# Decoder block on one core: the cross-attention's probabilities turned by a transposing DMA instead of by TensorE

## The chip, the cores and the metric

The kernel runs on one core of one Trainium2 chip. The metric is the device time of one execution in microseconds. Engines are called PE (TensorE, with PEld for its weight loads), DVE (VectorE), ACT (ScalarE), POOL (GpSimd) and SP (SyncE, which here only issues DMAs).

## The reference

One decoder block over x of 32 x 64 tokens of 256 values, in three parts, each on a layer norm and with a residual: a self-attention with quantised weights (16 heads of 16), a cross-attention onto a context of 32 x 64 x 128, and a mixture of 8 experts of which each token takes 2. The change lies in the cross-attention:

```python
q = (hidden_states @ Wq).reshape(B, Sq, H, D)          # H = 16 heads, D = 128
k = (encoder_hidden_states @ Wk).reshape(B, Skv, H, D)
v = (encoder_hidden_states @ Wv).reshape(B, Skv, H, D)
q = rmsnorm(q, gq); k = rmsnorm(k, gk)
scores = jnp.einsum('bqhd,bkhd->bhqk', q, k) * scale
attn = jax.nn.softmax(scores, axis=-1)
out = jnp.einsum('bhqk,bkhd->bqhd', attn, v)
return out.reshape(B, Sq, H * D) @ Wo
```

## The kernel before

The kernel has three stages one after the other: attention, cross_attention and experts. Each is written as one list of instructions for each engine, and semaphores order the lists against each other. Matrix products that need more than half precision are made from a high and a low f16 half of each factor, in three terms (TERMS).

In cross_attention the 32 sequences are cut into 4 groups of 8 (NG = 4, 512 tokens, GN). A group has 16 heads, and the work goes over pairs of heads: NPAIR = 32 pairs, 8 a group (NU). The loop variable is N, from -9 to 32. In step N the engines work on several pairs at once:

- PE makes the queries and keys of pair m = N + 9 (query, key and squares, L1209, L1217, L1229), the scores of pair n = N + 1 (scores, L1257), the outputs of the two heads of pair N (attend, L1291) and their way through the output weights (project_out, L1304). Values and output weights were multiplied beforehand, so attend multiplies the probabilities with the context itself.
- DVE turns the scores of pair N + 1 into differences to their maximum (shifted, L1119 to L1123) and sums their exponentials (sums, L1128 to L1132). It makes the low halves of queries (L1099), keys (L1103, L1105) and outputs (out_low, L1109), and of one piece of the experts' weights (L1142).
- ACT makes the exponential (L936), the high halves (out_high, L912, and others), and the copies out of PSUM.
- POOL divides by the sums (quotient, L848) and makes the low half of the probabilities (quotient_low, L853, which raises pl_done), besides products of norms (L841) and one weight piece (L857, L859).
- SP loads and saves pieces of the experts' weights (piece_load, piece_save, L790, L794), and sends the norms of the keys out and back in (L802, L816). It waits in order, so a wait at the head of its step holds up all that stands behind.

Steps 0 to 23 (N < TAIL = 24) are called full here; nearly all of them also make queries and keys. Steps 24 to 31 have only the rest of the attention to do.

PE's order in a full step is: scores(N+1), query(2m), key(2m), turn_p(N), project_out(2N-1), attend(2N), query(2m+1), squares(2m), key(2m+1), project_out(2N), attend(2N+1), squares(2m+1).

For attend the probabilities must lie with the keys on the partitions. turn_p(N) (L1271) does this with eight 128x128 transposes on PE, four blocks of each half, into the PSUM bank that also takes the scores (bank_s), and ACT copies the bank to pT in SBUF (turned_copy, L932). attend(2N) waits for that copy, and scores wait for it before they write the bank again. attend(h) also waits for ol_done, and project_out(h) for the low half of output h.

The experts' stage already turns its inputs by transposing DMAs on SP: rows_in (128x512 f16, L1515) and hid_hl (128x1536 f16, L1522).

Of the kernel before, what the change touches and what calls it, by code (L numbers as in the profile page):

```python
# [7 lines left out]
F16 = mybir.dt.float16  # L8
# [9 lines left out]
P = 128  # L18
# [641 lines left out]
def cross_attention(nc, sem, over, dram, x_sb, cst, ao, hT, wq, wk, wvo, cT, ck, carry, k_hl):  # L660
# [6 lines left out]
    with ctx:  # L667
# [11 lines left out]
        den = [sb(f"x_den{i}", [P, 2 * GT], F32) for i in range(2)]  # L679
        rden = [sb(f"x_rden{i}", [P, 2 * GT], F32) for i in range(2)]  # L680
        p_hl = [sb(f"x_p{i}", [P, 2, GN], F16) for i in range(2)]
        pT = sb("x_pT", [P, 2, 2, 2, P], F16)
        o_hl = [sb(f"x_o{i}", [P, 2, GN], F16) for i in range(2)]
        identh = carry.identh
        qk = pb("xbank_qk", [P, 2, 512], F32)
# [76 lines left out]
        def ob_of(h):  # L762
            return qk if h >= 2 * TAIL - 1 and h % 2 else ob

        def bank_of(n):
            return bank_s if n <= TAIL else bank_n

# [11 lines left out]
        with nc.Block() as block:  # L779

            @block.sync
            def _(sp):
                sp.dma_start(gains[:, 0:1], dram["gq2"].rearrange("(p a) -> p a", a=1)).then_inc(g_in, 16)
                sp.dma_start(gains[:, 1:2], dram["gk2"].rearrange("(p a) -> p a", a=1)).then_inc(g_in, 16)
                def piece_load(i):
                    if i == early:

                        sp.wait_ge(q_done, H2)
                        sp.wait_ge(k_done, H2)
                    sp.dma_start(raw(i), dram["wx"][:, i * PIECE:(i + 1) * PIECE]).then_inc(raw_in[i % 4], 16)  # L790

                def piece_save(i):
                    sp.wait_ge(low_odd if i % 2 else low_even, i // 2 + 1)
                    sp.dma_start(dram["w_hl"][:, :, i * PIECE:(i + 1) * PIECE].rearrange("l p n -> p l n"), halves(i)).then_inc(pair_out[i % 4], 16)  # L794
                    if loaded_behind(i) is not None:
                        piece_load(loaded_behind(i))

                def key_norms_out(b):
                    g, first = b * HB // H2, b * HB % H2
                    sp.wait_ge(kc_done, b + 1)  # L800
                    for t in range(GT):
                        sp.dma_start(dram["key_norms"][g % 2].rearrange("b h t s -> t h b s")[t, first:first + HB],  # L802
                                     kc[32 * t + first:32 * t + first + HB, :].rearrange("h (b s) -> h b s", b=2)).then_inc(kc_saved, 16)

                def key_norms_in(b, part):
                    g, first = b * HB // H2, b * HB % H2
                    sp.wait_ge(kc_saved, (b + 1) * GT * 16)
                    if g:
                        sp.wait_ge(s_read, (b * HB - H2 + HB) // 2)
                    if b == 1:  # L810

                        for r in range(4):
                            sp.wait_ge(pair_out[r], early // 4 * 16)
                    for u in range(first // 2 + 2 * part, first // 2 + 2 * part + 2):
                        for w in range(2):
                            sp.dma_start(rec_k[w * S:w * S + S, 2 * u:2 * u + 2, :].rearrange("p h c -> p (h c)"),  # L816
                                         dram["key_norms"][g % 2, w, 2 * u:2 * u + 2].rearrange("h t s -> (h t s)").partition_broadcast(S)).then_inc(rk_in[u], 16)

                for i in range(4):
                    piece_load(i)  # L820
                for N in steps:
                    for r in range(2):
                        if piece(piece_at(N, r)):
                            piece_save(piece_at(N, r))
                    if batch(N) is not None:
                        key_norms_out(batch(N))
                    for part in range(2):
                        if batch(N - 1 - part) is not None:
                            key_norms_in(batch(N - 1 - part), part)
                for r in range(4):  # L830
                    sp.wait_ge(pair_out[r], (NPIECE + 3 - r) // 4 * 16)
# [64 lines left out]
            def _(act):  # L896
# [31 lines left out]
                                         ACT.Exp, scale=-0.5, bias=gains[:, 4:5]).then_inc(rq_done, 1)  # L928

                def turned_copy(n):  # L930
                    act.wait_ge(t_done, n + 1)
                    nc.scalar.copy(pT[:, :, :, :, :].rearrange("p e l a n -> p (e l a n)"), bank_s[:, :].bitcast(F16)).then_inc(pT_done, 1)  # L932

                def exponent(n):
                    act.wait_ge(sub_done, n + 1)
# [1 line left out]

                def quotient_high(n):
                    act.wait_ge(pf_done, n + 1)
                    nc.scalar.copy(p_hl[n % 2][:, 0, :], pf[:, :, :].rearrange("p a s -> p (a s)")).then_inc(ph_done, 1)  # L940

                def piece_high(i):
# [44 lines left out]
                for N in steps:  # L987
# [22 lines left out]
                        query_norms(batch(N))  # L1010
                    if pair(m):
                        key(2 * m)
                    if pair(N):
                        turned_copy(N)
                    if pair(n):
                        exponent(n)
                    if pair(N):
# [184 lines left out]
            def _(pe):  # L1202
# [35 lines left out]
                def scores(n):  # L1238
                    pe.wait_ge(lq_done, n * 2 + 2)
                    pe.wait_ge(lk_done, n * 2 + 2)  # L1240
                    if n == 1:
                        pe.wait_ge(s_read, 1)
                    if 1 < n <= TAIL:
                        pe.wait_ge(pT_done, n - 1)
                    if n == TAIL + 1:

                        pe.wait_ge(rq_done, NHEAD // HB)
# [11 lines left out]

                def turn_p(n):  # L1260
                    pe.wait_ge(pl_done, n + 1)
                    if n < TAIL:

                        pe.wait_ge(s_read, n + 2)
                    else:
                        pe.wait_ge(pT_done, n)
                    for e in range(2):
                        for l in range(2):
                            for a in range(2):
                                at = (e * 2 + l) * 2 + a  # L1270
                                last = nc.tensor.transpose(bank_s[:, :].bitcast(F16)[:, at * P:(at + 1) * P], p_hl[n % 2][:, l, e * RW + a * P:e * RW + (a + 1) * P], identh[:, :])  # L1271
                    last.then_inc(t_done, 1)

                def attend(h):
                    pe.wait_ge(pT_done, h // 2 + 1)
                    if h == 2 * TAIL - 1:

                        pe.wait_ge(lq_done, NHEAD)
# [6 lines left out]
                    for a in range(2):  # L1285
                        for b in range(2):
                            for j, (l, m) in enumerate(TERMS):
                                for half in range(2):
                                    rows = slice(half * S, half * S + S)
                                    at = (2 * a + b) * S  # L1290
                                    last = nc.tensor.matmul(bank[:, half, at:at + S], ck[rows, l, h // H2 * 2 + a, b * CC:(b + 1) * CC],  # L1291
                                                            pT[rows, h % 2, m, a, b * S:b * S + S], start=(j == 0), stop=(j == 2))
                    last.then_inc(o_done, 1)

                def project_out(h):
# [44 lines left out]
                for N in steps:  # L1340
# [32 lines left out]
                        turn_hidden(6)  # L1373
                    if m == 6:
                        turn_hidden(7)
                    if pair(N):
                        turn_p(N)
                    if head(2 * N - 1):
                        project_out(2 * N - 1)
                    if pair(N):  # L1380
# [569 lines left out]
```

## Time and profile before

| | us |
|---|---|
| median of 3 runs | 901.29 |
| lowest, highest | 898.33, 901.67 |
| the profiled execution | 901.22 |
| its span, first to last instruction | 899.4 |
| mean granted TensorE clock | 0.936 of full speed |
| PE busy | 759.5 (84%) |
| DVE busy | 610.2 (68%) |
| ACT busy | 492.5 (55%) |
| POOL busy | 381.7 (42%) |

Busy times are sums over the span. Matmuls overlap in the pipeline, so a busy PE is not one at its peak. The full steps of the cross-attention lie from about 282 to 538 us, the experts' stage behind 597 us.

### The profile page before, as it was taken

How to read it: one execution, taken by the hardware profiler on the slowest of the kernel's cores; microseconds unless marked ns; L12 is line 12 of the kernel's file. 1: busy time of each engine (PE TensorE's matmuls, PEld its weight loads, DVE VectorE, ACT ScalarE, POOL GpSimd, SP SyncE). 2: the span in 40 equal slices, each digit the busy share in tenths (PEclk: the TensorE clock that was granted, in tenths of full speed). 3: DMA queues.
4: the chain of work that ended last, by engine and by line, in shares of the span. 5: the costliest groups of instructions: out<-in, count | busy, mean ns of one | idle time of the engine just before them, and what ended most of it. 6: DMA issues, size and time to landing. Idle time of an engine off the chain costs nothing. (4 is left out here: it accounts for less than half of the span.)

```text
span 899.4 us, 27604 instructions
## 1 busy us (share of the span) xinstructions
PE 759.5 (84%) x11193; PEld 544.5 (61%) x11193; DVE 610.2 (68%) x1069; ACT 492.5 (55%) x923; POOL 381.7 (42%) x446
## 2 busy tenths in 40 slices
PE   0498888887888999899999996985479999999991
PEld 0497787885444666566656665855247777777770
DVE  6778898864899999899999997967723333333330
ACT  0677777764877777676767764533023333333330
POOL 0123222222356555455555556510225666656642
PEclk9889988886999999999999997997689999999996
DMA  9100000001365333333334443149958899988874
GB/s 324 66 27 26 28 30 22 26 27 34 121 200 158 127 120 119 120 119 120 118 120 120 120 126 100 39 147 420 399 99 141 144 144 144 144 138 149 142 114 119
DMA packets 141226, 112.37 MB, mean 125 GB/s; under 512 B 88592, under 2 KB 121488, under 8 KB 140912
## 3 DMA queue, kind: packets, MB, share of 16 engines
q1 hardware_dynamic: 124672, 88.32, 36.8%
q0 software_dynamic: 7488, 10.23, 7.5%
q10 hardware_dynamic: 8944, 12.06, 3.9%
q8 instruction: 93, 1.52, 0.7%
q14 instruction: 29, 0.24, 0.1%
HBM read 63.13 MB, written 29.10 MB: 103 GB/s over the span
## 5 line engine op out<-in xcount | busy, mean ns | idle before, releaser
L1747 DVE SCALAR_TENSOR_TENSOR f_slot_work<-psu,f_slot_work 128x688 f32<-128x688 f32 x39 | 34.1, 874 | 124.0 <-PE psu L1818 124.0
L1304 PE MATMUL xbank_a<-arena,x_o 128*128 128x256 f16 x768 | 96.8, 277 | 8.1 <-DVE x_o L1109 6.4
L1566 POOL DMA_INDIRECT token_out<-f_y,f_to x39 | 62.2, 1594 | 79.9 <-ACT f_y L1622 54.3
L1304 PEld LDWEIGHTS xbank_a<-arena,x_o 128*128 128x128 f16 x768 | 71.8, 99 | 28.5 <-DVE x_o L1109 17.7
L1209 PE MATMUL xbank_qk<-arena 128*128 128x512 f16 x336 | 83.5, 385 | 1.7 <-DVE q_hl L1099 1.7
L1818 PE MATMUL psg<-wgu,f_slot_work 128*128 x468 | 76.7, 315 | 9.2 <-DMA f_slot_work<-rows_in 9.2
L1835 PE MATMUL fbank<-arena,f_slot_work 128*128 (+1 forms) x663 | 82.7, 273 | 0.5 <-DMA f_slot_work<-hid_hl 0.5
L848 POOL TENSOR_TENSOR x_pf<-x_sc,x_rden 128x512 f32<-128x512 f32 x32 | 33.4, 1042 | 108.3 <-DVE x_rden L1132 108.3
L1835 PEld LDWEIGHTS fbank<-arena,f_slot_work 128*128 128x128 f16 (+1 forms) x663 | 64.4, 97 | 18.9 <-issue 8.9
L1818 PE MATMUL psu<-wgu,f_slot_work 128*128 x468 | 75.1, 310 | 0.0
L1614 ACT CAST hid_hl<-f_slot_work 128x688 f16<-128x688 f32 x39 | 29.8, 765 | 77.8 <-DVE f_slot_work L1747 77.8
L901 ACT ACTIVATE sqq<-xbank_qk 128x512 f32<-128x512 f32 x56 | 33.3, 595 | 58.1 <-PE xbank_qk L1209 58.1
L1607 ACT ACTIVATE f_slot_work<-psg 128x688 f32<-128x688 f32 x39 | 29.0, 743 | 65.8 <-PE psg L1818 63.0
L1818 PEld LDWEIGHTS psg<-wgu,f_slot_work 128*128 128x128 f16 x468 | 43.2, 99 | 33.9 <-issue 10.0
L1818 PEld LDWEIGHTS psu<-wgu,f_slot_work 128*128 128x128 f16 x468 | 46.0, 98 | 22.9
L1750 DVE TENSOR_TENSOR hid_hl<-f_slot_work,hid_hl 128x688 f16<-128x688 f32 x39 | 34.1, 875 | 32.4 <-ACT hid_hl L1614 32.4
L528 PE MATMUL bank_pt<-cst,sp 64*64 64x64 f32 x1024 | 43.1, 244 | 14.3 <-ACT pT L289 13.7
L208 POOL TENSOR_SCALAR kd<-cst,deq 128x128 f32<-128x128 f32 x16 | 12.2, 764 | 95.6 <-PE bank_g L574 67.0
L1109 DVE SCALAR_TENSOR_TENSOR x_o<-xbank_o,x_o 128x512 f16<-128x512 f32 x55 | 37.7, 685 | 17.3 <-ACT x_o L912 17.3
L528 PEld LDWEIGHTS bank_pt<-cst,sp 64*64 64x64 f32 x1024 | 38.9, 156 | 16.3 <-issue 14.7
L1209 PEld LDWEIGHTS xbank_qk<-arena 128*128 128x128 f16 x336 | 28.6, 98 | 32.7 <-DVE q_hl L1099 2.5
L1217 PE MATMUL xbank_qk<-cT,wk 128*128 128x512 f16 x168 | 46.0, 383 | 0.0
(297 smaller groups left out, 1880.9 us busy)
## 6 DMA issues: line engine op xcount, KB each, us to landing
arena<-in_wx SPq DMA_DIRECT2D x51, 256.0 KB, 3.9
wgu<-w_hl SPq DMA_DIRECT2D x2, 5504.0 KB, 29.9
ao<-key_norms SPq DMA_DIRECT2D x64, 128.0 KB, 3.8
w_hl<-cT SPq DMA_DIRECT2D x26, 256.0 KB, 2.1
w_hl<-x_pair SPq DMA_DIRECT2D x25, 256.0 KB, 3.3
arena<-w_hl ACTq DMA_DIRECT2D x1, 3072.0 KB, 19.9
ao<-in_wx SPq DMA_DIRECT2D x10, 256.0 KB, 3.7
w_hl<-ao SPq DMA_DIRECT2D x10, 256.0 KB, 2.6
```

The lines of the kernel that those rows point to most:

```text
L528: last = nc.tensor.matmul(pt[rows, n * S:(n + 1) * S], sp[i % 2][rows, 8 * part + n, :], cst[rows, IDENT + S * b:IDENT + S * b + S], start ...
L848: nc.gpsimd.tensor_tensor(pf[:, :, :], sc[n % 2][:, :, :], rden[n % 2][:, :].unsqueeze(2).to_broadcast([P, 2 * GT, S]), ALU.mult).then_inc ...
L901: nc.scalar.activation(sqq[h % 2][:, :], query_bank(h), ACT.Square, scale=1.0 / (H_UP * W_UP)).then_inc(sq_done, 1)
L1109: nc.vector.scalar_tensor_tensor(out=o_hl[h % 2][:, 1, :].rearrange("p (b n) -> p b n", b=2), in0=ob_of(h)[:, :, 0:RW], scalar=1.0 / P_UP, ...
L1209: last = nc.tensor.matmul(query_bank(h), wq[:, a, k, f:f + D2], hT[:, g, b * NCH + k, :], start=(j == 0), stop=(j == len(terms) - 1))
L1217: last = nc.tensor.matmul(key_bank(h), wk[:, a, f:f + D2], cT[:, g, b, :], start=(j == 0), stop=(j == 2))
L1304: last = nc.tensor.matmul(acc[t // 2][:, (t % 2) * C:(t % 2 + 1) * C], o_hl[h % 2][:, a, at:at + P], wvo[:, b, e, :], start=(e == 0 and j ...
L1566: nc.gpsimd.indirect_dma_start(out=dram["token_out"], out_offset=bass.IndirectOffsetOnAxis(ap=to[n % 2][:, 0:1], axis=0), in_=y[n % 2][:, ...
L1747: nc.vector.scalar_tensor_tensor(out=h3, in0=psu[:, :].rearrange("p (c n) -> p c n", c=2)[:, :, 0:FH], scalar=HID_UP / (H_UP * W_UP), in1= ...
L1750: nc.vector.tensor_tensor(hid_hl[n % 2][:, 1, 0:FF], hid[n % 2][:, :], hid_hl[n % 2][:, 0, 0:FF], ALU.subtract).then_inc(s["hh_low"], 1)
L1818: last = nc.tensor.matmul(bank[:, c * 512:c * 512 + FH], xT[n % 2][:, b * NCH + k, :], wgu[:, bass.ds(e, 1), at:at + FH].rearrange("p a n ...
L1835: last = nc.tensor.matmul(ps[n % 2][:, 0:C], hidT[n % 3][0:rows, a, f, :], wd[0:rows, bass.ds(e, 1), at:at + C].rearrange("p a n -> p (a n)"),
```

## The change

The full steps' probabilities are turned by one DMA a pair, issued on SP at the head of SP's step N. The PE transposes and the ACT copy of these steps are gone; the eight tail steps keep them. The DMA has two destination buffers. The second lies in hT[:, 1], the hidden states of group 1, which are no longer read once the queries of that group are made; it takes the odd pairs from pair 9 on, and pT_first takes all others. Each parity of the pair has a semaphore of its own (turned_in). The order of the blocks in a buffer is changed from (head, half) to (half, head). scores(n) now waits only until the scores before are read (s_read), and quotient_high(n) waits until the transposition of pair n - 2 has read its buffer.

```diff
-        pT = sb("x_pT", [P, 2, 2, 2, P], F16)
+        pT_first = sb("x_pT", [P, 2, 2, 2, P], F16)
+        pT_second = hT[:, 1].rearrange("p j n -> p (j n)")[:, 0:8 * P].rearrange("p (l e a n) -> p l e a n", l=2, e=2, a=2)
+        turned_in = [sem(f"x_turned_in{i}") for i in range(2)]
...
+        def second(n):
+            return n % 2 == 1 and NU < n < TAIL
+
+        def pT_of(n):
+            return pT_second if second(n) else pT_first
+
+        def reader_before(n):
+
+            return max((k for k in range(n) if second(k) == second(n)), default=-1)
+
+        def turned_count(n):
+            return 16 * (n // 2 + 1)
...
+                def turn_p(n):
+                    sp.wait_ge(pl_done, n + 1)
+                    if reader_before(n) >= 0:
+                        sp.wait_ge(o_done, 2 * reader_before(n) + 2)
+                    if second(n):
+                        sp.wait_ge(q_done, 2 * H2)
+                    sp.dma_start(pT_of(n)[:, :, :, :, :].rearrange("p l e a n -> p (l e a) n"), p_hl[n % 2][:, :, :].rearrange("p l n -> p (l n)"), transpose=True).then_inc(turned_in[n % 2], 16)
+
                 for N in steps:
+                    if pair(N) and N < TAIL:
+                        turn_p(N)
                     for r in range(2):
...
                 def quotient_high(n):
                     act.wait_ge(pf_done, n + 1)
+                    if 2 <= n < TAIL + 2:
+                        act.wait_ge(turned_in[n % 2], turned_count(n - 2))
...
-                    if pair(N):
-                        turned_copy(N)
                     if pair(n):
                         exponent(n)
...
-                    if n == 1:
-                        pe.wait_ge(s_read, 1)
-                    if 1 < n <= TAIL:
-                        pe.wait_ge(pT_done, n - 1)
+                    if 1 <= n <= TAIL:
+                        pe.wait_ge(s_read, n)
...
                 def attend(h):
-                    pe.wait_ge(pT_done, h // 2 + 1)
+                    if h < 2 * TAIL:
+                        pe.wait_ge(turned_in[h // 2 % 2], turned_count(h // 2))
+                    else:
+                        pe.wait_ge(pT_done, h // 2 - TAIL + 1)
...
-                    if pair(N):
-                        turn_p(N)
                     if head(2 * N - 1):
                         project_out(2 * N - 1)
```

## Rows read from the trace of the kernel before

**Rows 1.** The page: TensorE's granted clock, in tenths, in 40 slices.

```profile
PEclk9889988886999999999999997997689999999996
```

**Rows 2.** Windows: window, length, busy PE, PEld, DVE, ACT, POOL (count), clock, DMA share.

```profile
392.00:478.00 86.00, 82.16 (x1383) 52.12 (x1380) 79.17 (x121) 60.58 (x108) 45.22 (x40) 1.00 0.38 120
```

**Rows 3.** Timeline of DVE in one full step, its window, all of L1123.

```profile
413.68 0.69 DVE L1109 SCALAR_TENSOR_TENSOR x_o<-xbank_o,x_o 128x512 f16<-128x512 f32 x1 [0.41 <-ACT x_o L912]
414.50 0.69 DVE L1119 TENSOR_TENSOR x_sc<-xbank_s,ao 128x512 f32<-128x512 f32 x1
...
421.12 0.68 DVE L1109 SCALAR_TENSOR_TENSOR x_o<-xbank_o,x_o 128x512 f16<-128x512 f32 x1
...
424.48 0.69 DVE L1109 SCALAR_TENSOR_TENSOR x_o<-xbank_o,x_o 128x512 f16<-128x512 f32 x1 [0.58 <-ACT x_o L912]
...
414.50:421.10 6.60, 6.43 (x77) 3.70 (x77) 6.42 (x10) 4.30 (x8) 2.40 (x2) 1.00 0.29 90
...
L1123 DVE TENSOR_TENSOR x_sc<-x_sc,x_mx x22: 691/1578/1649, 305.9 to 536.1; 128x512 f32<-128x512 f32 x22
```

**Rows 4.** Timeline of PE and ACT in the same step.

```profile
416.35 0.61 PE L1271 MATMUL xbank_s<-identh,x_p 128*128 128x128 f16 x8
...
416.79 1.47 PE L1304 MATMUL xbank_a<-arena,x_o 128*128 128x256 f16 x12
...
418.43 0.52 PE L1291 MATMUL xbank_o<-x_pT,ck 64*128 64x64 f16 x24 [0.17 <-ACT x_pT L932]
...
421.86 1.49 PE L1304 MATMUL xbank_a<-arena,x_o 128*128 128x256 f16 x12 [0.17 <-DVE x_o L1109]
...
423.28 0.52 PE L1291 MATMUL xbank_o<-x_pT,ck 64*128 64x64 f16 x24
...
423.85 0.60 ACT L912 ACTIVATE x_o<-xbank_o 128x512 f16<-128x512 f32 x1 [0.33 <-PE xbank_o L1291]
```

**Rows 5.** The same step: POOL's x_p, SP's first issue, a window.

```profile
412.51 1.16 POOL L853 TENSOR_TENSOR x_p<-x_pf,x_p 128x512 f16<-128x512 f32 x1
...
418.16 0.38 SPq L794 DMA_DIRECT2D w_hl<-cT  x1
...
413.70:417.70 4.00, 4.00 (x74) 2.79 (x69) 3.80 (x5) 2.27 (x5) 2.65 (x2) 1.00 0.00 0
```

**Rows 6.** Timeline of the experts' stage: transposing DMAs and their waiters.

```profile
656.35 1.20 SPq L1515 DMA_TRANSPOSE f_slot_work<-rows_in  x1
...
658.82 0.18 POOL L1548 COPY f_at<-f_from_all 128x1 uint32<-128x1 uint32 x1 [0.44 <-DMA f_slot_work<-rows_in]
...
873.86 1.42 SPq L1522 DMA_TRANSPOSE f_slot_work<-hid_hl  x1
...
877.77 2.14 PE L1835 MATMUL fbank<-arena,f_slot_work 128*128 x17 [0.54 <-DMA f_slot_work<-hid_hl]
...
693.14 1.19 SPq L1515 DMA_TRANSPOSE f_slot_work<-rows_in  x1
...
698.87 0.18 POOL L1548 COPY f_at<-f_from_all 128x1 uint32<-128x1 uint32 x1 [0.49 <-DMA f_slot_work<-rows_in]
```

**Rows 7.** Timeline of steps 0 and 23 and the step behind.

```profile
282.66 1.17 POOL L853 TENSOR_TENSOR x_p<-x_pf,x_p 128x512 f16<-128x512 f32 x1
...
287.05 0.52 PE L1291 MATMUL xbank_o<-x_pT,ck 64*128 64x64 f16 x24 [1.48 <-ACT x_pT L932]
...
532.67 1.16 POOL L853 TENSOR_TENSOR x_p<-x_pf,x_p 128x512 f16<-128x512 f32 x1
...
537.34 0.53 PE L1291 MATMUL xbank_o<-x_pT,ck 64*128 64x64 f16 x24
...
542.80 1.03 PE L1271 MATMUL xbank_s<-identh,x_p 128*128 128x128 f16 x8 [3.71 <-POOL x_p L853]
```

**Rows 8.** Windows of the filling steps and of the attention stage.

```profile
274.00:278.00 4.00, 2.43 (x14) 0.84 (x10) 3.90 (x7) 2.98 (x8) 2.21 (x2) 1.00 0.06 21
132.00:133.00 1.00, 0.00 (x0) 0.00 (x0) 1.00 (x1) 0.94 (x6) 1.00 (x1) 0.61 0.00 0
```

More of the change, by code:

```diff
@@ L930, in turned_copy @@
                 def turned_copy(n):
-                    act.wait_ge(t_done, n + 1)
-                    nc.scalar.copy(pT[:, :, :, :, :].rearrange("p e l a n -> p (e l a n)"), bank_s[:, :].bitcast(F16)).then_inc(pT_done, 1)
+                    act.wait_ge(t_done, n - TAIL + 1)
+                    nc.scalar.copy(pT_first[:, :, :, :, :].rearrange("p l e a n -> p (l e a n)"), bank_s[:, :].bitcast(F16)).then_inc(pT_done, 1)
                 def exponent(n):
@@ L1261, in turn_p @@
                     pe.wait_ge(pl_done, n + 1)
-                    if n < TAIL:
-                        pe.wait_ge(s_read, n + 2)
+                    if n == TAIL:
+                        pe.wait_ge(s_read, TAIL + 1)
                     else:
-                        pe.wait_ge(pT_done, n)
+                        pe.wait_ge(pT_done, n - TAIL)
                     for e in range(2):
@@ L1269, in turn_p @@
                             for a in range(2):
-                                at = (e * 2 + l) * 2 + a
+                                at = (l * 2 + e) * 2 + a
                                 last = nc.tensor.transpose(bank_s[:, :].bitcast(F16)[:, at * P:(at + 1) * P], p_hl[n % 2][:, l, e * RW + a * P:e * RW + (a + 1) * P], identh[:, :])
@@ L1291, in attend @@
                                     last = nc.tensor.matmul(bank[:, half, at:at + S], ck[rows, l, h // H2 * 2 + a, b * CC:(b + 1) * CC],
-                                                            pT[rows, h % 2, m, a, b * S:b * S + S], start=(j == 0), stop=(j == 2))
+                                                            pT_of(h // 2)[rows, m, h % 2, a, b * S:b * S + S], start=(j == 0), stop=(j == 2))
                     last.then_inc(o_done, 1)
```

## The prediction

> **What bounds the kernel now.** I read the page first, for where the stage lies and at what clock TensorE runs in it [rows 1]: slices 14 to 24 of the forty, where PE and DVE show eights and nines, are the stage that the change touches, and the granted clock is nine tenths or more there. The view by windows over 86 us of it has PE busy 82.16 us, DVE 79.17 and ACT 60.58 [rows 2]. PE at 96% and DVE at 92% are too close for shares to decide, and a busy PE in this view is not one at its peak. So I laid out one full step (one pair of heads, N in the code) in order of time, first DVE, then PE.
>
> DVE first [rows 3]. A step repeats after 10.80 us: out_low(2N+1) at 413.68 and again at 424.48. The scores are read at 414.50 (L1119), and from there to out_low(2N) at 421.12 DVE works its list without a pause: 6.42 us busy in a window of 6.60 us, and the 0.18 us left over are the hand-overs between dependent instructions. The 1.58 us of L1123 belong to that list. Both times out_low(2N+1) had to wait, 0.41 and 0.58 us, for ScalarE's out_high (L912).
>
> PE after that [rows 4]. Behind out_low(2N), which ends at 421.12 + 0.68 = 421.80, project_out(2N) starts at 421.86, attend(2N+1) at 423.28, ScalarE's out_high(2N+1) at 423.85, DVE's out_low(2N+1) at 424.48. So the loop that sets the step is: DVE list 6.62 us (414.50 to 421.12), out_low 0.68, hand-over 0.06, project_out 1.42 to the start of attend, attend with hand-over 0.57, ScalarE 0.63, then out_low(2N+1) 0.69 and 0.13 to the next L1119: 6.62 + 0.68 + 0.06 + 1.42 + 0.57 + 0.63 + 0.69 + 0.13 = 10.80 us. In it PE has no part but project_out(2N) and attend(2N+1), in the second half. The eight transposes (start 416.35) and the first attend (418.43) lie in the first half, beside the DVE list. PE paid for them with its own slack only: project_out(2N) is released by DVE's out_low after 0.17 us of idle PE.
>
> **What the change removes.** In each of the 24 full steps the eight PE transposes go. They hold PE from 416.35 to the start of project_out(2N-1) at 416.79, so 0.44 us [rows 4]. The wait of attend(2N) for ScalarE's copy, 0.17 us, goes too if the DMA is in time. PE thus comes to project_out(2N) some 0.6 us earlier and finds out_low(2N) not done: its idle time there grows from 0.17 to about 0.8 us. Worth on the path: 0. Without that cover it would be 24 x 0.61 = 14.6 us.
>
> ScalarE loses one copy of 128x1024 a step, which runs between the last transpose and attend(2N). Its result is only wanted by attend. The work behind it on ScalarE is the exponent and out_high(2N), and DVE takes both only when its list, gapless as it is, comes to them. Worth: 0. Also 0 are the freed score bank (scores(N+1) waits for an older reader than before, but PE arrives there late, behind squares and attend(2N+1), at the end of the loop), the second buffer, and the new wait of quotient_high for a transposition two steps old, 21 us back. The wait for the queries of the second group is over by step 9, the first that uses the second buffer (the last of those queries is made in step 6).
>
> **What it adds.** One transposing DMA of 128x1024 f16 (256 KB, eight blocks) on SP's queue, at the head of SP's step, after pl_done(N). That is the end of x_p's low half on POOL: 412.51 + 1.16 = 413.67 [rows 5]. The other wait, for the reader of the same buffer, is met earlier: attend(2N-1) starts a period before the 423.28 of attend(2N+1), at 412.48, and hands over within 0.57 us, by 413.05. From step 10 on the reader is two steps back.
>
> How late may it land? attend(2N) started at 418.43 with 0.17 us to spare before project_out(2N) had its input, so up to 418.60 costs nothing: a budget of 418.60 - 413.67 = 4.93 us. PE itself would now be at attend(2N) at 418.43 - 0.61 = 417.8, 4.15 us after pl_done.
>
> How long does it take? The trace has transposing DMAs in the experts' stage only [rows 6]. 128 KB on nearly idle engines: issued 656.35, its waiter on POOL starts at 658.82: 2.47 us. 384 KB beside a scatter: issued 873.86, its waiter on PE starts at 877.77: 3.91 us. 128 KB beside the DMAs of the other slots: 693.14 to 698.87: 5.73 us. In the full steps the engines are idle when the transposition would run: the DMA share is 0.00 over 413.7 to 417.7 [rows 5]. So I interpolate between the first two: (2.47 + 3.91) / 2 = 3.2 us. Bounds are 2.5 and 5.7 us. At 3.2 us it lands at 416.9, 0.9 us before PE arrives and 1.7 us inside the budget. I take 0 per step; the upper bound gives 5.73 - 4.93 = 0.80 us a step, 19 us in all.
>
> The Trainium skill ("VectorE: DVE Perf Modes", section "The three transpose paths") speaks against the change: it gives 1309 ns for one 128x128 block through the DMA crossbar against 390 ns on TensorE, and advises TensorE where the result may go to PSUM. Eight blocks one after another would be 10.5 us by that page, an estimate, and the sum would be 901.3 + 24 x (10.5 - 4.9) = some 1035 us. The row of 384 KB, twelve blocks in 3.91 us with issue and landing, disagrees with such an addition.
>
> What stands behind the new instruction on SP: the two saves and two loads of weight pieces and, in two steps of four, the four loads of key norms. The first of them is issued at 418.16 [rows 5], when DVE has the even piece ready, while the transposition's issue (1.20 to 1.42 us [rows 6]) is over by 415.2. Nothing is held up: 0.
>
> **The edges.** Step 0: x_p is ready at 282.66 + 1.17 = 283.83 and attend(0) starts at 287.05 after a wait of 1.48 us for the copy [rows 7]. With 3.2 us the DMA lands at 287.1: 0 to +0.3 us. Step 23, which has no query and key projections to hide behind: x_p at 532.67 + 1.16 = 533.83, attend(46) at 537.34 [rows 7]. The DMA lands at 537.1, and attend(46) starts then, 0.2 us earlier; it is worth 0, for PE stands idle 3.71 us a little later, until POOL has the next x_p at 542.8. The eight tail steps keep the old way.
>
> **The sum.** Profiled execution 901.22 us (span 899.4, 1.8 around it), which is the median of the three runs, 901.29, to 0.1. Removed on the path 0, added 0, edges 0 +- 0.3: **901.3 us**.
>
> **Rivals.**
> A. PE's time counts after all, because DVE's list has slack that the view does not show. For it: PE is busy 96% and out_low waits 0.4 to 0.6 us in each step. Against it: these waits lie behind project_out(2N), which starts 0.06 us after DVE's out_low ends. Full price -14.6 us: 886.6. If only a part counts, 890 to 897. Put under A as well: DVE's L1123 takes 1.58 us in the median and 0.69 at its shortest [rows 3]. Were it always short, that would be 24 x 0.89 = -21 us, 880; but nothing that starts DVE's or POOL's instructions there moves.
> B. (the other side) The transposition lands late and its wait takes the place of the copy's. It decides from 4.93 us after pl_done; each 0.25 us beyond is 6 us on the total, so 907 at 5.2 us and 920 at the 5.73 us of the loaded row. For it: the trace has no transposition of 256 KB, and the key norms' DMAs end only a few us before. Against it: idle engines in the very window.
> C. PE idles more and the granted clock falls to the lower level. In the filling steps 4 us with PE busy 2.43 keep 1.00, while a drop (0.61 in that us) comes in a stretch without any PE work [rows 8]. The new idle pieces are some 0.8 us long. If the whole stage ran at half the clock, its PE work, 10.0 us a step, would double: at least 24 x 9 = +216 us, 1117.
> D. The blocks of one transposition are done one after another, each at the price of the loaded row: 5.73 / 4 = 1.43 us. Eight would take 11.5 us, 6.5 beyond the budget: +157 us, 1058. Against it stands the row of twelve blocks in 3.91 us. (The Trainium skill's "VectorE: DVE Perf Modes", named above, has a block price of that size; the trace disagrees with its addition.)
> That the DMA isn't made, or that the old way stays, can't be: the code for N < TAIL has no other.
>
> **Chances.** No change 0.70, A 0.12, B 0.14, C 0.03, D 0.01. A measurement of this kernel can tell about 0.5%, 4.5 us, from no change; its three runs spread over 3.3 us. The likeliest case's own range is 898 to 905. Range for 8 in 10: all of it, the mild half of A and of B: 894 to 908. Faster by over 0.5%: 0.12; within: 0.71; slower: 0.17.
>
> **What would show it.** Right: the step still repeats after 10.8 us; DVE busy 6.4 of 6.6 us between L1119 and out_low(2N); PE's idle time before project_out(2N) grown to about 0.8 us with DVE's out_low as releaser; attend(2N) with no wait, or a short one, for the transposing DMA; landing 3 to 3.5 us after x_p. Wrong: attend's waits for the DMA longer than 0.8 us (B), a step shorter than 10.5 us (A), a granted clock under 1.00 in these slices (C). The prediction fails most easily on the one size that has no row, the landing of 256 KB, and on the reading that DVE's list has no slack.

## The result and the profile after

| | before | after |
|---|---|---|
| median of 11 runs each, us | 899.02 | 896.02 |
| lowest, us | 896.73 | 894.11 |
| the profiled execution, its span, us | 901.22, 899.4 | 894.42, 892.6 |

The ratio is 0.9967, with a 95% interval of 0.9954 to 0.998: the changed kernel is faster by 0.33%. That is under the 0.5% which the prediction named as the least that can be told, but more runs than the three of before told it. One of the eleven runs of the kernel before, 1019.67 us, was a slow one, which the ratio leaves out. Of the 5.3 us between forecast and measurement, 2.3 us are the kernel before, which took 899.02 us in these runs and not 901.29; 3.0 us are the change.

The page after, beside [rows 1]: busy times, the granted clock, and two DMA queues (packets, MB, share).

```profile
PE 744.8 (83%) x11001; PEld 530.0 (59%) x11001; DVE 607.6 (68%) x1069; ACT 472.3 (53%) x899; POOL 382.7 (43%) x446
...
PEclk9999888886999999999999998997689999999996
...
q1 hardware_dynamic: 150016, 94.62, 42.7%
...
q8 instruction: 92, 1.51, 0.7%
```

PE lost 192 matmuls and as many weight loads, ScalarE 24 copies, 20.2 us of busy time. The clock is nine tenths or more in the stage, so rival C is out. The last line becomes important below: q8 brings in instructions, one packet of 16 KB at a time (1.51 MB / 92).

One full step after: DVE, timeline, beside [rows 3].

```profile
411.21 0.69 DVE L1144 TENSOR_TENSOR x_sc<-xbank_s,ao 128x512 f32<-128x512 f32 x1
411.93 0.69 DVE L1146 TENSOR_REDUCE x_mx<-x_sc 128x8 f32<-128x512 f32 x1
412.65 1.58 DVE L1148 TENSOR_TENSOR x_sc<-x_sc,x_mx 128x512 f32<-128x512 f32 x1
414.16 0.68 DVE L1167 SCALAR_TENSOR_TENSOR cT<-arena,cT 128x512 f16<-128x512 f32 x1
...
417.82 0.68 DVE L1134 SCALAR_TENSOR_TENSOR x_o<-xbank_o,x_o 128x512 f16<-128x512 f32 x1
...
421.18 0.69 DVE L1134 SCALAR_TENSOR_TENSOR x_o<-xbank_o,x_o 128x512 f16<-128x512 f32 x1 [0.63 <-ACT x_o L937]
422.00 0.69 DVE L1144 TENSOR_TENSOR x_sc<-xbank_s,ao 128x512 f32<-128x512 f32 x1
```

The scores are read at 411.21 and again at 422.00: 10.79 us, as before (10.80). The list from there to out_low(2N) takes 417.82 - 411.21 = 6.61 us (6.62 before). L1148 is the old L1123, still 1.58 us.

The same step on PE, beside [rows 4].

```profile
414.46 0.52 PE L1317 MATMUL xbank_o<-x_pT,ck 64*128 64x64 f16 x24
415.49 1.47 PE L1234 MATMUL xbank_qk<-arena 128*128 128x512 f16 x6 [0.51 <-DVE q_hl L1124]
...
418.56 1.49 PE L1330 MATMUL xbank_a<-arena,x_o 128*128 128x256 f16 x12 [0.27 <-DVE x_o L1134]
419.98 0.52 PE L1317 MATMUL xbank_o<-x_pT,ck 64*128 64x64 f16 x24
```

attend(2N) comes 3.25 us behind the read of the scores (3.93 before), without a wait. The freed time came out as idle time, 0.51 us ahead of the next query and 0.27 us ahead of project_out(2N): 0.78 us in all, where the prediction had 0.8, but all of it ahead of project_out(2N). In this step the loop therefore did what was forecast. To find the 3 us I cut the two profiled executions into stages by their first and last instructions: the 24 full steps (from the first read of the scores to the 25th) took 260.50 us before and 258.84 after, the tail up to the statistics 62.09 and 60.20, the experts' slots (first to last sigmoid-weighted gate on ScalarE) 208.74 and 207.38. These two executions differ by more than the medians, 6.8 us in the span, and 2.5 us of that lie ahead of the first full step (274.15 and 271.61 us), where nothing was changed. Two single places hold the differences of tail and slots.

Place 1, the tail's third step, whose scores are read 546.64 and 557.70 before (11.06 us), 542.45 and 551.60 after (9.15 us). Before: SP's load of a weight piece, ScalarE's wait for it.

```profile
551.16 2.08 SPq L790 DMA_DIRECT2D arena<-in_wx  x1
...
555.94 0.63 ACT L948 ACTIVATE cT<-arena 128x512 f16<-128x512 f32 x1 [5.59 <-DMA arena<-in_wx]
```

After:

```profile
546.97 0.47 SPq L805 DMA_DIRECT2D arena<-in_wx  x1
...
549.84 0.63 ACT L975 ACTIVATE cT<-arena 128x512 f16<-128x512 f32 x1 [3.68 <-DMA arena<-in_wx]
```

The same load is issued in 2.08 us before and in 0.47 us after; ScalarE and everything behind it waits 1.91 us less. The DMA view of the kernel before for 550.5 to 552.0 us names who else is there (an instruction packet, and no such line for 546.0 to 547.5 us after):

```profile
q8 instruction: 1, 0.02, 6.2%
...
arena<-in_wx SPq DMA_DIRECT2D x1, 256.0 KB, 4.8
```

Place 2, the third slot of the experts: 4.86 us from gate to gate before, 3.50 us after. Before, the turned rows come late for PE:

```profile
668.05 1.19 SPq L1515 DMA_TRANSPOSE f_slot_work<-rows_in  x1
...
672.69 1.92 PE L1818 MATMUL psg<-wgu,f_slot_work 128*128 x12 [1.22 <-DMA f_slot_work<-rows_in]
```

After, the same DMA issued at 662.12 is waited for by nobody on PE. Here too the DMA view has an instruction packet in the kernel before, 1.5 us behind the issue, and none after.

### The profile page after: what moved, and what is told of

Read it like the earlier page. It is cut to its first block and busy times, and to the rows that moved or that the text cites. A ratio compares the mean times of both kernels' runs of the same rounds, so it can differ in the third digit from the quotient of the medians.

```text
span 892.6 us, 27243 instructions
## 1 busy us (share of the span) xinstructions
PE 744.8 (83%) x11001; PEld 530.0 (59%) x11001; DVE 607.6 (68%) x1069; ACT 472.3 (53%) x899; POOL 382.7 (43%) x446
## 3 DMA queue, kind: packets, MB, share of 16 engines
q8 instruction: 92, 1.51, 0.7%
```

## The experiments

My first theory, from these two places: PE's instruction stream is 384 instructions shorter by the tail (192 matmuls and 192 weight loads). The packets therefore fall at other moments (one and a half packets, if a packet holds 256 instructions, as the page of the Trainium skill named below has it), and no longer beside two DMAs whose landing is on the path. Against it stood: PE's and ScalarE's freed time, the transposing DMA itself, and chance.

All runs in one table: median, ratio to the kernel before among the same runs with its 95% interval, and from the profile the 24 full steps, the tail's third step and the experts' third slot.

| kernel | us | ratio | steps | tail | slot |
|---|---|---|---|---|---|
| before | 899.02 | 1 | 260.50 | 11.06 | 4.86 |
| before_again | 898.87 (one run) | | 259.73 | 10.15 | 5.20 |
| after | 896.02 | 0.9967 (0.9954 to 0.998) | 258.84 | 9.15 | 3.50 |
| after_again | 896.82 | 0.996 (0.9944 to 0.9976) | 258.58 | 9.14 | 3.50 |
| no_turn | 896.41 | 0.997 (0.9952 to 0.9989) | 257.08 | 9.15 | 3.50 |
| dma_alone | 898.25 | 0.9978 (0.9959 to 0.9998) | 259.93 | 10.35 | 4.90 |
| dma_alone2 | 900.64 | 1.0007 (0.9989 to 1.0025) | 259.78 | 9.93 | 4.95 |
| pad_before | 897.44 | 0.9986 (0.9968 to 1.0003) | 259.47 | 9.16 | 3.50 |
| pad_after | 897.08 | 0.9972 (0.9958 to 0.9986) | 256.42 | 10.04 | 3.50 |
| pad2_before | 899.49 | 0.9997 (0.9977 to 1.0016) | 262.27 | 9.66 | 4.97 |
| pad2_after | 896.70 | 0.9966 (0.9949 to 0.9983) | 257.85 | 9.12 | 3.50 |
| port_before | 892.77 | 0.9919 (0.9896 to 0.9942) | 254.15 | 9.78 | 5.05 |
| port_after | 889.88 | 0.9883 (0.9859 to 0.9907) | 250.41 | 9.10 | 3.50 |
| port2_before | 892.57 | 0.9927 (0.9907 to 0.9948) | 251.36 | 10.22 | 4.80 |
| port2_after | 886.84 | 0.9869 (0.9843 to 0.9895) | 247.31 | 9.24 | 3.50 |
| late_in | 898.94 | 0.9994 (0.9975 to 1.0013) | 260.09 | 9.18 | 3.50 |
| late_out | 905.15 | 1.0065 (1.0043 to 1.0087) | 266.48 | 9.16 | 3.50 |

### The two kernels once more, and each half of the change

after_again and before_again are the two kernels unchanged.

> The changed kernel once more, for a second trace. Its first trace keeps the full step at 10.79 to 10.80 us, yet its median is 3.0 us under the kernel before. Theory S (steps): the loop through DVE is unchanged and the 3 us come from single places: late loads of weight pieces in steps 9, 22 and 27, and stages outside the cross-attention, where two executions of one kernel differ as much. Then the places differ from trace to trace and the period stays 10.80. Theory R (real, at an edge): the same places gain again, above all the tail step 27, where 1.9 us were gained. Ratio to before in both 0.995 to 0.999.

> The kernel before once more, for a second trace. Theory S: the steps with a late weight piece lie elsewhere than in its first trace (steps 9 and 27), the period is 10.8 us elsewhere, and the attention stage differs from the first trace by 1 to 3 us. Theory R: step 27 is again some 2 us longer than in the changed kernel.

no_turn has neither the transposes nor the DMA: each later full pair's attend reads the probabilities that were turned in step 0.

```diff
                     if pair(m):
                         key(2 * m)
-                    if pair(N):
+                    if N == 0:
                         turned_copy(N)
...
-                    pe.wait_ge(pT_done, h // 2 + 1)
+                    pe.wait_ge(pT_done, 1 if h < 2 * TAIL else h // 2 - TAIL + 2)
```

> The kernel before without the PE transposes and ACT copies of the full steps 1 to 23; attend reads the probabilities that step 0 turned, so the output is not the reference's. No DMA takes their place. If DVE sets the step as predicted: period 10.8 us, time within 0.3% of before, that is 897 to 901 us. If PE's 0.6 us a step count: 885 us. If the 3 us of the change come from the freed PE and ACT time, this shows them too, with 895 to 897 us.

dma_alone (and later dma_alone2, the same) is the kernel before with the new DMA for pairs 9 to 23 beside the old way, into a buffer that nobody reads.

```diff
+                    if NU < N < TAIL:
+                        turn_p(N)
```

> The kernel before with all its work, and beside it the transposing DMA of pairs 9 to 23 into the second buffer, which nobody reads (15 of the 24, for there is no room for the first nine). If DMA and queue cost nothing: 899 us, period 10.8. If the DMA delays pieces or engines: over 900 us, with DMA waits of ACT for pieces. If the DMA in some way brings the gain (for instance by moving the loads of pieces): 895 to 897 us.

Leaving the turning out altogether gains no more than moving it to the DMA: 0.997 against 0.996 and 0.9967. So the DMA costs nothing beyond these intervals, about 2 us on the whole (single late landings do cost something, below), and the gain belongs to the removal. Most steps repeat after 10.79 to 10.80 us in all of them. What goes with the removal in these profiles is the tail's third step and the slot. dma_alone was unclear: its profile has both stalls, its ratio was a little below 1. The repetition below gives 1.0007.

### Where the instruction packets fall

pad_before and pad_after put 64 tiny matmuls ahead of PE's first work, where it waits for data until 13.57 us anyway: 128 instructions, half a packet.

```diff
+                pad = cst[:, 0:P].bitcast(F16)
+                for i in range(64):
+                    nc.tensor.matmul(kb[:, 0:4], pad[:, 0:P], pad[:, P:P + 4], start=True, stop=True)
```

> The kernel before with 64 tiny matmuls (64 weight loads and 64 matmuls of 4 columns) ahead of its first work on PE, into a bank that is written afterwards; 128 PE instructions more, about 5 us of PE at the most, in a time in which PE waits for its first data. Nothing else is changed. Theory 1 (the place of the instruction loads): the packets of 16 KB by which instructions are brought in come once per 256 PE instructions, so they now fall half a period elsewhere. Then the one beside SP's load in the tail goes: the 27th step from its scores to the next takes 9.15 us in place of 10.2 to 11.1, and the third slot of the experts 3.50 us in place of 4.9 to 5.2. In all 1 to 3 us less than before, 896 to 898 us, ratio 0.996 to 0.999. Theory 2 (the gain is PE's and ScalarE's freed time, or the freed copy): nothing moves, 899 to 900 us, and both steps keep their old lengths.

> The changed kernel with the same 64 tiny matmuls ahead of its first work on PE. Theory 1 (the place of the instruction loads): the packets fall near where they fell before, so the 27th step takes 10 us or more again and the third slot of the experts about 4.9 us; 898 to 900 us, ratio to the kernel before 0.999 to 1.001. Theory 2 (freed time of PE and ScalarE): the gain stays, 896 to 897 us, ratio 0.996 to 0.997, the 27th step at 9.15 us and the third slot at 3.50 us.

pad2_before and pad2_after have 128 of them, a whole packet.

> The kernel before with 128 tiny matmuls ahead of its first work on PE: 256 PE instructions, a whole period of the instruction loads, so that these fall where they fell before. It is the control of pad_before. Theory 1 (the place of the instruction loads): the tail's 27th step takes 10.2 to 11.1 us again and the third slot of the experts 4.9 to 5.2 us; 899 to 900 us, ratio 0.999 to 1.001. Theory 2 (the tiny matmuls did something of their own, such as a warmer PE): both stay at 9.15 and 3.50 us, as in pad_before, 897 us.

> The changed kernel with 128 tiny matmuls, a whole period. Theory 1 (the place of the instruction loads): 9.15 us for the 27th step and 3.50 us for the third slot as in the changed kernel; 896 to 897 us, ratio 0.996 to 0.997. Theory 2 (any padding costs something): 897 to 898 us, like pad_after.

> The kernel before with transposing DMAs of pairs 9 to 23 into a buffer that nobody reads, once more, since its first ratio of 0.9978 left open whether the DMA by itself gains something. Theory 1 (place of the instruction loads, and steps that PE without transposes can shorten): neither is changed, ratio 0.999 to 1.001, the 27th step above 10 us and the third slot 4.9 us. Theory 2 (the DMA beside the old way gains by itself): ratio 0.998 or less again.

In the tail theory 1 held in all four. The padding by half a packet freed the kernel before (9.16 us) and loaded the changed one (10.04 us); the whole packet did neither (9.66 and 9.12 us). This is pad_after, the changed kernel with the stall put back: the issue is long, ScalarE waits 0.9 us more.

```profile
546.43 1.28 SPq L808 DMA_DIRECT2D arena<-in_wx  x1
...
550.19 0.63 ACT L978 ACTIVATE cT<-arena 128x512 f16<-128x512 f32 x1 [4.56 <-DMA arena<-in_wx]
```

The DMA view in windows of 0.1 us gives each packet's place. In eight of the 17 profiles a packet lies between 0.5 us ahead of the start of this load's issue and 0.5 us behind it; the step takes 9.66 to 11.06 us in them (mean 10.15), and the issue 0.89 to 2.08 us in seven of the eight. In the nine others no packet is there, the issue takes 0.47 us and the step 9.10 to 9.24 (mean 9.16). The price of this place is 1.0 us. The same holds for the weight loads of the whole cross-attention in all 17 profiles: without a packet within 0.5 us of its start the issue took more than 0.6 us in 23 of 786 cases, with one in 48 of 81. The number of q8's packets follows PE's instructions too: 93 before, 94 in both of its paddings, 92 after.

The expectation for pad_after failed in two points: its slot took 3.50 us, not 4.9, and its time came out at 897.08 us, ratio 0.9972, and not at 898 to 900. By the time alone theory 2 (896 to 897 us) would have been nearer. The positions account for the slot. In the seven profiles with the long slot (4.80 to 5.20 us) a packet follows the issue of the rows' DMA by 1.4 to 2.1 us. In pad_after it follows by 2.3 us, and the rows were no longer delayed; in pad_before, and in the profiles without PE transposes other than pad_after, there is none. In pad_before the rows of the next slot came late instead: issued at 665.81 us, they reached PE at 671.42, with a packet 3.4 us behind their issue, and that slot took 6.48 us in place of 5.57. How near a packet must lie to delay a landing is therefore not told by these profiles. So pad_before gave back 0.9 us of what it gained, and pad_after lost only the tail: the ratios of both lie between those of the two kernels, where the whole packets reproduce these (0.9997 and 0.9966). The intervals of the half paddings overlap, so single medians don't separate them; the steps in the profiles do.

The Trainium skill, "Runtime: NRT & Kernel Launch", section "Instruction fetch mechanics", says that instructions are refilled in blocks of 16 KiB, 256 instructions, and that crossing a block is mostly hidden. The size agrees with q8's packets. For the DMAs issued beside it the fetch was not hidden: the load's issue took 0.89 to 2.08 us in place of 0.47 in seven profiles. What it cost PE itself no row here shows.

### What the change is worth when DVE's list is shorter

Rival A rested on slack in DVE's list, L1123's 1.58 us above all. In the traces of both kernels it takes that long where POOL's second operation on its weight piece has started before it (412.53 to 413.69 us beside the list above), and 0.69 us where it starts first itself (in the kernel before at 295.01, POOL 0.01 us later) or where POOL's second operation comes later still. That holds for all 391 of these subtractions in steps 1 to 23 of the 17 profiles: 1.57 to 1.68 us in 221 of them, 0.69 us in 168 of the 170 others. port_before and port_after hold POOL's piece until DVE has the block maximum; port2_before and port2_after until DVE has done its own weight piece too.

```diff
                     n, m = N + 1, N + AHEAD
+                    if pair(n) and N < TAIL:
+                        pool.wait_ge(mx_done, n + 1)
```

```diff
+                        if piece(piece_at(N, 0)):
+                            pool.wait_ge(low_even, piece_at(N, 0) // 2 + 1)
+                        else:
+                            pool.wait_ge(mx_done, n + 1)
```

> The kernel before, with one wait more on POOL: in a full step whose successor begins a pair, POOL holds its next weight piece until DVE has left the block maximum of the step after. This keeps POOL's two-input operation off the time in which DVE's two-input operations on SBUF take 1.58 us instead of 0.7. Theory 1 (DVE's list holds a recoverable collision of about 0.9 us a step, and PE with its eight transposes is the next limit): full steps of about 10.3 us in place of 10.80, 24 x 0.5 = 12 us less, 887 us, range 884 to 892. Theory 2 (the list has no slack to be had, or POOL's piece then comes late): steps of 10.80 us or more, 899 us or above.

> The changed kernel with the same wait on POOL. Theory 1: without the collision the step is set by PE, which has no transposes here: steps of about 9.95 us, 24 x 0.85 = 20 us less than the changed kernel, 877 us, range 873 to 883, and so 8 to 10 us under the kernel before with the same wait: this is what the change is worth where DVE no longer sets the step. Theory 2 (no recoverable collision): 896 us or above. Theory 3 (collision gone, but the transposes' 0.44 us a step were hidden on PE all the same): the same time as the kernel before with this wait, within 2 us.

The collision was recoverable, but both sizes were off: steps of 10.45 and 10.32 us (10.3 and 9.95 expected), so the change was worth 0.13 us a step. In port_after DVE's list is still the bound, 6.15 us with the weight piece at 1.10 us beside POOL's:

```profile
410.05 0.69 DVE L1146 TENSOR_TENSOR x_sc<-xbank_s,ao 128x512 f32<-128x512 f32 x1
...
411.50 0.69 DVE L1150 TENSOR_TENSOR x_sc<-x_sc,x_mx 128x512 f32<-128x512 f32 x1
...
412.11 1.10 DVE L1169 SCALAR_TENSOR_TENSOR cT<-arena,cT 128x512 f16<-128x512 f32 x1
...
416.20 0.68 DVE L1136 SCALAR_TENSOR_TENSOR x_o<-xbank_o,x_o 128x512 f16<-128x512 f32 x1
```

6.15 us and the same 4.17 us behind it are 10.32. That gave the next two expectations.

> The kernel before with POOL's next weight piece held until DVE has finished its own weight piece of the step (in place of the block maximum, as in port_before). In port_before DVE's piece still took 1.10 us beside POOL's, and 0.68 without it, but there PE, with its eight transposes a step, went without a pause. Theory 1 (PE with the transposes sets 10.44 us there): the 0.42 us taken from DVE's list are worth nothing, steps stay at 10.4 to 10.45 us, 892 to 893 us. Theory 2 (DVE's list still sets the step): 10.0 us, 24 x 0.4 = 10 us less, 883 us.

> The changed kernel with the same hold on POOL. In port_after the step of 10.32 us is DVE's list of 6.15 us and the same 4.17 us behind it as in the kernel before, with PE idle 0.28 us ahead of project_out. Theory 1 (DVE's list still sets it, PE has some 0.3 us of room without the transposes): the list falls by 0.42 to 5.7 us and PE takes over at 10.32 - 0.28 = 10.0 us; 22 x 0.3 = 7 us less than port_after, 883 us, range 881 to 886. The change is then worth some 0.4 us a step, 9 to 10 us, against the kernel before with the same hold. Theory 2 (PE limits both at 10.3 to 10.4 us): 889 to 890 us, and the change is worth 3 us at any length of DVE's list.

Now the steps came close to the expectations: 10.45 us with the transposes, 9.90 to 9.91 without (10.0 expected). port2_after's time, 886.84 us, lies above its range of 881 to 886. The windows of one such step, columns as in [rows 2], first port2_before:

```profile
418.41:428.86 10.45, 10.28 (x179) 6.71 (x179) 9.13 (x16) 7.42 (x13) 5.86 (x5) 1.00 0.51 158
```

then port2_after:

```profile
477.16:487.06 9.90, 9.90 (x172) 6.31 (x171) 9.12 (x15) 7.02 (x15) 5.83 (x5) 1.00 0.64 137
```

PE is busy 10.28 us and waits 0.17 us for ScalarE's copy in the first, and works without any pause in the second. PE is now the bound, and the change is worth 0.38 us of PE's work (10.28 - 9.90) and the 0.17 us of waiting, 0.55 us a step, against 0.61 in the prediction for the case without cover. Yet the medians differ by 5.7 us, not 24 x 0.55 = 13. Four of the steps could gain nothing: 0, 1, 9 and 17 take 9.0, 10.5, 11.1 and 11.1 us in both. port2_after's other rows tell where 6.3 us more went: attend waits for late transpositions.

```profile
383.14 1.24 SPq L840 DMA_TRANSPOSE x_pT<-x_p  x1
...
389.68 0.52 PE L1322 MATMUL xbank_o<-x_pT,ck 64*128 64x64 f16 x24 [2.42 <-DMA x_pT<-x_p]
```

This landing took 6.54 us, with an instruction packet 2.2 us behind the issue; that step lasted 12.25 us. Three more late landings (5.47, 5.72 and 4.72 us; behind the second a packet lies only at 3.6 us) made steps of 11.13, 12.09 and 10.43 us: together 2.35 + 1.23 + 2.19 + 0.53 = 6.3 us over 9.90.

### How late may the transposition land?

late_in and late_out issue the DMA of steps 0 to 22 only behind DVE's read of the next scores (s_read), or behind its maximum (mx_done).

```diff
+                    if n + 1 < TAIL:
+                        sp.wait_ge(s_read, n + 2)
                     sp.dma_start(pT_of(n)...
```

> The changed kernel with each transposition of steps 0 to 22 issued only after DVE has read the next pair's scores, some 1.5 us later than x_p is ready. It then lands 3.15 us after that, 3.9 us behind the start of the read; attend(2N) may start 4.1 us behind it (418.60 - 414.50 in the kernel before). Theory 1 (the budget of 4.93 us behind x_p holds): the step stays 10.80 us and the time 896 to 897 us. Theory 2 (the budget is smaller, PE must come to attend earlier): steps over 10.9 us and 900 us or more.

> The changed kernel with each transposition of steps 0 to 22 issued only after DVE's block maximum, 0.72 us later again. It lands 4.6 us behind the start of the read of the scores, 0.5 us after the budget. Theory 1: a new loop sets the step: read of the scores and maximum 1.45 us, landing 3.15, attend(2N) and the queries and keys up to project_out(2N) 3.3, project_out 1.42, attend and hand-over 0.57, ScalarE 0.63, out_low and hand-over 0.82: 11.3 us, 23 x 0.5 = 12 us more, 908 us, range 903 to 915. Theory 2 (PE's time freed by the transposes covers it): 10.80 us and 896 to 897 us.

late_in kept its step of 10.79 us, with attend waiting some 0.5 us, though its median came out at 898.94, 2 us above the expectation; its interval reaches down to 0.9975 and its profile shows only 1.3 us more in the full steps than after's. late_out has the new loop in every step, 11.09 to 11.13 us (11.3 expected) and 905.15 us (908). On PE and SP in late_out:

```profile
418.64 1.24 SPq L842 DMA_TRANSPOSE x_pT<-x_p  x1
```

```profile
421.74 0.52 PE L1319 MATMUL xbank_o<-x_pT,ck 64*128 64x64 f16 x24 [1.28 <-DMA x_pT<-x_p]
424.83 1.47 PE L1332 MATMUL xbank_a<-arena,x_o 128*128 128x256 f16 x12
```

The landing is 3.10 us, 4.60 us behind the start of the read of the scores at 417.14. That costs 0.3 us a step, and late_in's 3.88 us (412.71 + 3.10 - 411.93) cost nothing. So attend may come some 4.3 us behind the read, where the prediction had 4.1 (418.60 - 414.50): rival B's mechanism exists, and its budget was right to 0.2 us.

## Why the prediction was right, and where it failed

- The loop of 10.80 us was right in each of its parts for most steps: period 10.79, DVE's list 6.61, PE's freed 0.78 us turned into waits for DVE. Taking DVE's list away (port2) moved the bound to PE, as that reading says.
- "Removed on the path 0" was right for most steps, not for all. Where a weight piece for ScalarE came late, POOL's piece moved and missed DVE's: "nothing that starts DVE's or POOL's instructions there moves" was too strong. The changed kernel shows one such step, on DVE and POOL:

```profile
510.67 1.49 POOL L882 TENSOR_SCALAR arena<-arena 128x512 f32<-128x512 f32 x1 [1.92 <-ACT x_pair L975]
511.02 0.80 DVE L1148 TENSOR_TENSOR x_sc<-x_sc,x_mx 128x512 f32<-128x512 f32 x1
512.24 1.20 POOL L884 TENSOR_TENSOR x_pair<-arena,x_pair 128x512 f16<-128x512 f32 x1
```

  That step took 10.01 us. Such steps mostly take 9.9 to 10.1 us without the transposes and 10.28 to 10.45 with them; the five profiles without transposes and without any hold have one to five of them, the six with transposes none or one. In the mean of these profiles the 24 full steps take 257.8 us without the transposes and 260.3 with them.
- The landing: 3.2 us were interpolated. Step 0 shows 3.21 us, step 23 3.09 us, all 24 of late_out 3.07 to 3.22 us (each to the start of the attend that waits for it). That is the undisturbed landing, and what the prediction said of steps 0 and 23 was right:

```profile
281.13 1.37 SPq L840 DMA_TRANSPOSE x_pT<-x_p  x1
```

```profile
284.34 0.52 PE L1317 MATMUL xbank_o<-x_pT,ck 64*128 64x64 f16 x24 [1.90 <-DMA x_pT<-x_p]
```

  "Landing 3 to 3.5 us after x_p" and "added 0" did not hold throughout. The profile's landing marks of the changed kernel's 24 transpositions (the view of L840):

```profile
DMA to landing us min/median/max: 3.0/3.6/5.3
```

  13 of the 24 took more than 3.5 us. Only one exceeded the budget of 4.93 us, and there attend waited 1.23 us, more than the 0.8 us that the prediction named as a sign of rival B. Five more attends waited 0.2 to 0.6 us. So B's mechanism was at work in one step in 24.

- The block-by-block price (rival D, and beside it the Trainium skill's 1309 ns) is refuted: eight blocks in 3.1 us are at most 0.39 us each, landing and issue included.
- **Two terms of the sum failed: "edges 0 +- 0.3", the claim that nothing outside the full steps moves, and "removed on the path 0".** For the first, the prediction looked for waits of the engines and of DMA queues that the kernel's own code issues. It had no term for the instruction packets, though the page lists them. In their place the runs showed two stalls of the kernel before, 1.0 us in the tail and 1.3 to 1.7 us in the experts' third slot, that went or came back with the position of the packets in four paddings, but for the slot of pad_after. In place of the second they showed single steps of 9.9 to 10.1 us, where POOL's piece misses DVE's and PE without its transposes is soon ready.

How the 3.0 us divide between the two is open. The stalls come to 2.4 us or so, the mean difference of the full steps to 2.5, together more than was measured. But the full steps together differ by over 2 us between profiles of kernels of one kind, and the first full step starts anywhere from 271.2 to 275.3 us in both kinds, which is more than the effect. pad_before and pad_after, whose profiles have about the same stalls (0.9 us in a slot against 1.0 in the tail), have medians only 0.4 us apart, which speaks for the packets as the larger part; their intervals overlap. Why a packet lengthens another DMA's issue and landing no trace shows; that the delay in the tail comes and goes with it is shown. late_in, which has neither stall and still measured 0.9994, fits only at the edge of its interval.

## What to carry to other kernels

Work taken off an engine that isn't the bound gives little where it was, but it shifts that engine's instruction stream; differences under half a per cent can then come from where the instruction packets fall. A padding of half a packet at the start, profiled on both kernels, shows which stalls move with the packets; the medians alone did not separate them here. Before work is moved off the second-busiest engine, look for what lengthens the first one's list: here one wait on POOL gained 6.6 us (899.35 to 892.77) where the change gained 3, and with the longer hold the change was worth 5.7 us (892.57 to 886.84). A transfer that is hidden at its usual landing wants a budget for its late ones too.

## What the runs showed of the hardware

- A transposing DMA of 128x1024 f16 within SBUF lands in 3.07 to 3.22 us. With an instruction packet 0.4 to 2.3 us behind its issue it mostly takes longer: in the six profiles with the DMA at its place, 68 of 76 such landings took more than 3.5 us by the profile's marks. 42 landings took more than 4.2 us, and 38 of these have such a packet. The changed kernel's longest, issued at 388.56 with a packet 1.5 us behind, and DVE's list in that step:

```profile
390.80 0.69 DVE L1148 TENSOR_TENSOR x_sc<-x_sc,x_mx 128x512 f32<-128x512 f32 x1
...
393.90 0.52 PE L1317 MATMUL xbank_o<-x_pT,ck 64*128 64x64 f16 x24 [1.23 <-DMA x_pT<-x_p]
```

  5.34 us, over the budget of 4.93. It fell in a step of 11.06 us (the scores are read at 389.35 and 400.41), which took 10.87 in the kernel before. L1148 is short there, as in the step of 10.01 us above; by that comparison, an estimate, the late landing cost about 1 us. In late_in, whose issue comes 1.5 us later, hardly any packet falls behind it, and 22 of 24 landings are 3.06 to 3.21 us.
- The issue of a weight piece's load on SP takes 0.47 us, and 0.89 to 2.08 us for the tail's load in seven of eight profiles in which a packet falls within 0.5 us of its start.
- DVE's subtraction of two SBUF operands takes 0.69 us alone or when it starts first, and 1.58 us when POOL's TENSOR_TENSOR started 0.12 us before it. The Trainium skill, "SBUF — State Buffer", section "Who interferes with whom", has it that DVE with two SBUF inputs contends with a GpSimd instruction that reads SBUF; the trace agrees, and shows 0.69 to 1.10 us beside POOL's TENSOR_SCALAR.
